# Own job lists for the first and last turns of a pipelined attention and feed-forward kernel on one core

## The chip, the core and the metric

The kernel runs on one core of one Trainium2 chip. The metric is the device time of one execution in microseconds. The engines are TensorE (PE, its weight loads PEld), VectorE (DVE), ScalarE (ACT), GpSimd (POOL) and SyncE (SP, which here only issues DMAs).

## The reference, cut to what matters

```python
def reference(x, w_qkv, b_qkv, w_out, b_out, W1, b1, W2, b2):   # x is (32, 512, 256)
    x = x + layernorm(attention(layernorm(x)))
    x = x + layernorm(relu(layernorm(x) @ W1 + b1) @ W2 + b2)
    return x
# attention: 16 heads of 16; scores = q k^T / 4 + mask; softmax; times v; times w_out
# mask: a query block of 128 rows sees its own block and block 0; block 0 sees all, all see block 0
# W1 is (256, 1024), W2 is (1024, 256), everything in float32
```

## The kernel before, in words

There are 32 batches of 512 rows. The work of one batch is cut into jobs: `x1` (transposes of the normalised input), `qk` 0 to 3 and `v` (projections), `scores_max` 0 to 19 (scores that only give a row maximum, by the DVE job `reduce`), `max_t` 0 to 3 (transposes of the maxima, copied by `copy_max`), `scores` 0 to 19 (scores again with the maximum as one more row, then `exp` on ACT), `pv` 0 to 3 (probabilities times values, read by ACT's `read_o`), `o_t`, `o2`, `op` (the output projection, read by DVE's `op_out`), `x2`, `f1` 0 to 7 and `f2` 0 to 3 (feed-forward). Each operand of a projection is held as a high and a low part (`_hi`, `_lo`), so ACT writes the high part and DVE (for h, POOL) the low one. `relu` on ACT writes h twice, `h_lo` on POOL subtracts. The layer norms are `_stats`, `_mean` (DVE), `_rstd` (POOL), `_shift`, `_apply`.

The scores' operands stand in the tile `stack`, to which SP copies q and k by 6 small DMAs for each of 8 head pairs (`load_stack` 0 to 7, line L323). The negative maxima go through DRAM: `store_row` 0 to 3 (L332) and `load_row` 0 to 3 (L336). SP issues its DMAs in order, and one that waits holds all behind it.

The order of the work is written out by hand in the table `ORDER`: one list for each engine, one turn of the pipeline, each entry a job, its number and the offset of its batch from the turn. On PE a fourth number names the pair of PSUM banks (`p_pair` 0 to 3) that the job writes; a job waits until the former user of its pair has been read out. A turn holds jobs of five batches at once. PE's program is unrolled. The other engines' programs are turns 0 to 5 written out, a loop, and the last turns written out. In the first and last turns the same list is used, and entries whose batch does not exist are left out (`there`).

The weights are loaded by SP into tiles that are free at the start and split by ACT (`w_hi`, L515 and L521) and DVE (`w_lo`, L587 and L594). POOL sets constant ones in `stack` and `values` by memsets (L726, L728) after the first layer norm's `_rstd`.

In the text a batch stands in brackets, counted from 0: max_t 0 (1) is job `max_t` 0 of the second batch.

## Time and profile before

| | us |
|---|---|
| median of 3 runs | 2061.07 (2060.56 to 2062.49) |
| profiled execution, its own time | 2061.84 |
| its span, first to last instruction | 2060.0 |

| engine | busy us | share of the span |
|---|---|---|
| PE | 1938.2 | 94% |
| PEld | 1588.0 | 77% |
| DVE | 1536.7 | 75% |
| ACT | 1408.6 | 68% |
| POOL | 722.8 | 35% |

The span is what the profiler's rows cover; 1.8 us of the execution's own time lie outside. The shares are means over a filling pipeline, a long steady middle and a draining pipeline, and the rows below take these apart. The mean granted TensorE clock was 0.977 of 2.4 GHz.

### The profile page before, as it was taken

The page shows a single profiled execution, that of the slowest core. Times are in us where ns is not written, and L with a number is a line of the kernel's source. Part 1 is how long each engine was busy: PE and PEld are TensorE (multiplying, and loading weights), DVE is VectorE, ACT ScalarE, POOL GpSimd, SP SyncE. Part 2 cuts the span into 40 slices and gives each one's busy share as a digit, 9 for nine tenths or more (in the row PEclk, how much of TensorE's full clock was granted, in tenths as well). Part 3 has the DMA queues.
Part 4 walks back from the last instruction along what each step waited for, and adds up shares of the span by engine and source line. Part 5 has one row for each costly group of instructions (what it writes and reads, how often), then busy time and mean ns, then how long its engine had stood idle before and what let it go on. Part 6 is the DMA issues. An engine that isn't in the chain of part 4 may idle for free. (4 is left out here: it accounts for less than half of the span.)

```text
span 2060.0 us, 70899 instructions
## 1 busy us (share of the span) xinstructions
PE 1938.2 (94%) x27904; PEld 1588.0 (77%) x27904; DVE 1536.7 (75%) x2916; ACT 1408.6 (68%) x2341; POOL 722.8 (35%) x905
## 2 busy tenths in 40 slices
PE   3879999999999999999999999999999999999985
PEld 2557887788888778888877888787788878778765
DVE  6577777777787777778777787877778787777631
ACT  2446677777777777777777776777777677777653
POOL 2013333333333333333333333333433334343343
PEclk8789999999999999999999999999999999999998
DMA  4343343334334333433433343343334334333200
GB/s 124 71 84 73 76 90 68 80 80 93 78 81 91 68 79 81 92 78 82 91 67 77 84 90 79 80 91 66 79 84 88 79 82 89 68 80 76 54 27 16
DMA packets 132817, 160.61 MB, mean 78 GB/s; under 512 B 29408, under 2 KB 82400, under 8 KB 132576
## 3 DMA queue, kind: packets, MB, share of 16 engines
q1 hardware_dynamic: 132048, 156.29, 35.8%
q8 instruction: 222, 3.64, 0.8%
q10 hardware_dynamic: 528, 0.52, 0.1%
q14 instruction: 19, 0.16, 0.0%
HBM read 38.21 MB, written 17.83 MB: 27 GB/s over the span
## 5 line engine op out<-in xcount | busy, mean ns | idle before, releaser
L613 DVE TENSOR_REDUCE max_bias<-p_pair 128x4 f32<-128x1024 f32 (+1 forms) x640 | 761.4, 1215 | 104.1 <-PE p_pair L363 87.9
L530 ACT ACTIVATE probs<-p_pair 128x1024 f32<-128x1024 f32 x640 | 638.8, 1027 | 246.4 <-PE p_pair L363 134.9
L746 POOL TENSOR_TENSOR h_lo<-h_f,h_hi 128x512 fp32r<-128x512 f32 x256 | 329.8, 1288 | 477.5 <-ACT h_hi L562 477.4
L366 PE MATMUL p_pair<-stack 49*128 49x256 f32 (+1 forms) x3072 | 352.3, 314 | 36.3 <-ACT probs L530 15.0
L562 ACT ACTIVATE h_f<-p_pair,b_s 128x256 f32<-128x256 f32 x512 | 247.9, 484 | 119.3 <-PE p_pair L393 119.3
L366 PEld LDWEIGHTS p_pair<-stack 49*128 49x128 f32 (+1 forms) x3072 | 241.3, 191 | 111.6 <-ACT probs L530 46.8
L393 PE MATMUL p_pair<-x_hi,w_hi 64*128 64x256 f32 (+1 forms) x2560 | 302.6, 308 | 13.0 <-DVE x_lo L625 5.5
L393 PE MATMUL p_pair<-w_hi,h_hi 64*128 64x256 f32 x2048 | 286.7, 277 | 10.0 <-POOL h_lo L746 7.4
L393 PE MATMUL p_pair<-x_hi,w_lo 64*128 64x256 f32 (+1 forms) x2560 | 295.9, 302 | 0.0
L393 PE MATMUL p_pair<-x_lo,w_hi 64*128 64x256 f32 (+1 forms) x2560 | 295.7, 302 | 0.0
L393 PE MATMUL p_pair<-w_lo,h_hi 64*128 64x256 f32 x2048 | 284.1, 274 | 0.0
L393 PE MATMUL p_pair<-w_hi,h_lo 64*128 64x256 f32 x2048 | 283.9, 274 | 0.0
L562 ACT ACTIVATE h_hi<-p_pair,b_s 128x256 fp32r<-128x256 f32 x512 | 249.1, 486 | 0.0
L363 PE MATMUL p_pair<-stack 49*128 49x512 f32 (+1 forms) x1024 | 220.2, 433 | 19.6 <-DMA stack<-qk 7.3
L393 PEld LDWEIGHTS p_pair<-x_hi,w_hi 64*128 64x128 f32 x2560 | 213.5, 187 | 24.1 <-DVE max_bias L613 13.0
L393 PEld LDWEIGHTS p_pair<-x_hi,w_lo 64*128 64x128 f32 x2560 | 215.8, 186 | 11.7
L393 PEld LDWEIGHTS p_pair<-x_lo,w_hi 64*128 64x128 f32 x2560 | 215.5, 186 | 11.7
L393 PEld LDWEIGHTS p_pair<-w_hi,h_hi 64*128 64x128 f32 x2048 | 192.9, 185 | 15.1 <-POOL h_lo L746 6.0
L432 PEld LDWEIGHTS p_pair<-probs,values 128*32 128x32 f32 x3072 | 106.3, 112 | 120.5 <-issue 81.0
L393 PEld LDWEIGHTS p_pair<-w_lo,h_hi 64*128 64x128 f32 x2048 | 193.1, 185 | 2.8
L432 PE MATMUL p_pair<-probs,values 128*32 128x256 f32 x3072 | 194.2, 385 | 0.0
L393 PEld LDWEIGHTS p_pair<-w_hi,h_lo 64*128 64x128 f32 x2048 | 192.7, 185 | 0.0
(77 smaller groups left out, 2815.6 us busy)
## 6 DMA issues: line engine op xcount, KB each, us to landing
stack<-qk SPq DMA_DIRECT2D x1536, 64.0 KB, 2.3
xr<-x SPq DMA_DIRECT2D x32, 512.0 KB, 4.0
out<-yf SPq DMA_DIRECT2D x64, 256.0 KB, 2.2
xa<-x SPq DMA_DIRECT2D x31, 512.0 KB, 4.5
shift_rows<-max_t SPq DMA_DIRECT2D x128, 8.0 KB, 1.3
stack<-shift_rows SPq DMA_DIRECT2D x128, 8.0 KB
...
```

Source lines behind the costliest of these rows:

```text
L363: last = nc.tensor.matmul(dst[:, j, :], stack[r, stationary, at, 0:P], stack[r, moving, at, :], start=True, stop=True)
L366: last = nc.tensor.matmul(dst[:, j, col:col + HALF].rearrange("p (a n) -> p a n", a=2), stack[r, stationary, at, kb * P:(kb + 1) * P], two ...
L393: last = nc.tensor.matmul(dst[:, u, cols], stationary(r), moving(r), start=part == 0 and at == 0 and m == 0, stop=part == 1 and m == adden ...
L432: last = nc.tensor.matmul(two(o, kb), v, probs[:, prob_slot(n, c), j, col:col + HALF] .rearrange("p (a n) -> p a n", a=2), start=False, st ...
L530: nc.scalar.activation(probs[:, prob_slot(quad, c), :, :], banks("scores", n)[:, :, :], ACT.Exp, scale=SCALE).then_inc(exp_done, 1)
L562: last = nc.scalar.activation(dst, banks("f1", n)[:, n % 2, u * HALF:(u + 1) * HALF], ACT.Relu, bias=b1_s[:, m:m + 1])
L613: nc.vector.tensor_reduce(dst, src, axis=AX.X, op=ALU.max, negate=True).then_inc(red_done, 1)
L746: nc.gpsimd.tensor_tensor(h_parts[1][:, m:m + 2, :], h_f[:, n % 2, :, :], h_parts[0][:, m:m + 2, :].bitcast(F32), ALU.subtract).then_inc(h ...
```

## The change

Each engine gets two more lists, `FIRST` and `LAST`, with jobs and batches written out one by one. `FIRST` stands in place of the thinned turns 0 to 3 and `LAST` in place of those after the last full turn (offsets there count from the end, -1 is the last batch). Full turns by `ORDER` run between them, 28 on PE. `ORDER` itself has other positions and other bank pairs. The jobs are the same ones; only the weight splits became jobs (`split_hi`, `split_lo`) with places in `FIRST`.

The first input comes in two halves, on ACT's and SP's queues. The weights after the first are issued from ACT's queue, each staged in a tile of its own. Of the low splits, the first stays on DVE and five go to POOL. The memset of one half of the `stack` ones runs at POOL's start, the other after both halves of the first batch are normalised.

```diff
+FIRST = {
+    "PE": [
+        ("x1", 0, 0), ("qk", 0, 0), ("qk", 1, 0), ("qk", 2, 0), ("qk", 3, 0), ("scores_max", 0, 0),
...
+        ("scores", 11, 0), ("scores", 12, 0), ("scores", 13, 0), ("o_t", 1, 0), ("scores", 14, 0),
+        ("max_t", 0, 1), ("scores", 15, 0), ("scores", 16, 0), ("pv", 2, 0), ("scores", 17, 0),
...
+    "POOL": [
+        ("ln1_rstd", 0, 0), ("ln1_rstd", 1, 0), ("ones", 0, 0), ("ln1_rstd", 0, 1), ("ones", 1, 0),
+        ("split_lo", 1, 0), ("split_lo", 2, 0), ("ln1_rstd", 1, 1), ("split_lo", 3, 0), ("ln1_rstd", 0, 2),
...
+LAST = {
+    "PE": [
...
+        ("scores", 19, -1), ("x2", 0, -2), ("o_t", 2, -1), ("pv", 3, -1), ("f1", 0, -2), ("f1", 2, -2),
+        ("f1", 1, -2), ("f1", 3, -2), ("o_t", 3, -1), ("o2", 0, -1), ("f1", 4, -2), ("f1", 6, -2),
+        ("f2", 0, -2), ("f1", 5, -2), ("f2", 1, -2), ("f1", 7, -2), ("op", 0, -1), ("op", 1, -1), ("f2", 2, -2),
+        ("f2", 3, -2), ("x2", 0, -1), ("f1", 0, -1), ("f1", 2, -1), ("f1", 1, -1), ("f1", 3, -1), ("f1", 4, -1),
+        ("f1", 6, -1), ("f2", 0, -1), ("f1", 5, -1), ("f2", 1, -1), ("f1", 7, -1), ("f2", 2, -1), ("f2", 3, -1),
...
+        W_STAGE = ((O_QKV, O_W1, probs[:, :, :, :].rearrange("p a u n -> p (a u n)")[:, 0:O_W1]),
+                   (O_WO, O_W2, h_f[:, :, :, :].rearrange("p a u n -> p (a u n)")[:, 0:KD * D]),
+                   (O_W1, O_W1 + F, ya[:, :, :].rearrange("p a n -> p (a n)")),
+                   (O_W1 + F, O_WO, o_n[:, :, :].rearrange("p a n -> p (a n)")),
+                   (O_W2, O_W2 + KB * D, x1_old[:, :, :].rearrange("p a n -> p (a n)")),
+                   (O_W2 + KB * D, WCOLS, yf[:, :, :].rearrange("p a n -> p (a n)")))
...
-            act.dma_start(xa[:, :, :], x_t[0]).then_inc(xa_in, 16)
+            act.dma_start(xa[:, 0:HB, :], x_t[0, :, 0:HB, :]).then_inc(xa_first, 16)
+            sp.dma_start(xa[:, HB:KB, :], x_t[0, :, HB:KB, :]).then_inc(xa_in, 16)
...
+                elif what == "split_lo":
+                    first_col, stop, stage = W_STAGE[n]
+                    pool.wait_ge(hi_split, n + 1)
+                    nc.gpsimd.tensor_tensor(w_lo[:, first_col:stop], stage, w_hi[:, first_col:stop].bitcast(F32),
+                                            ALU.subtract).then_inc(lo_rest, 1)
...
-                pool.wait_ge(rstd_done["ln1"], 2)
-                for j in range(2):
-                    nc.gpsimd.memset(stack[ROW * j + 32:ROW * (j + 1), 1, :, :].bitcast(F32), 1.0).then_inc(ones_set, 1)
-                    pool.wait_ge(ones_set, j + 1)
+            stack_ones(0)
+                if what == "ones" and n == 0:
+                    pool.wait_ge(norm_done["ln1"], 2)
+                    stack_ones(1)
```

What SP issues in batch 0 after the first loads stood so before (`stack<-qk x24` is `load_stack` for four pairs, `shift_rows<-max_t` is `store_row`, `stack<-shift_rows` is `load_row`):

```order
L323 DMA stack<-qk 16x2x512 x24
L332 DMA shift_rows<-max_t 16x128
L336 DMA stack<-shift_rows 2x2x512
L323 DMA stack<-qk 16x2x512 x24
L332 DMA shift_rows<-max_t 16x128
L345 DMA xa<-x 128x4x256
L336 DMA stack<-shift_rows 2x2x512
```

It stands so now:

```order
L530 DMA stack<-qk 16x2x512 x24
L539 DMA shift_rows<-max_t 16x128
L530 DMA stack<-qk 16x2x512 x6
L543 DMA stack<-shift_rows 2x2x512
L530 DMA stack<-qk 16x2x512 x6
L539 DMA shift_rows<-max_t 16x128
L530 DMA stack<-qk 16x2x512 x12
L543 DMA stack<-shift_rows 2x2x512
```

The second `store_row` moved from behind 24 DMAs of pairs 4 to 7 to behind 12 of them, and the pairs' loads stand between each store and its load.

In the middle turns PE had this around `pv` 2 (the last rows of `f2` 3 first; `stack` x2 or x4 is a `scores` or `scores_max` job, `probs,values` is `pv`, the number behind p_pair the bank pair):

```order
L393 MATMUL p_pair0<-w_hi,h_lo 128x256 x2
L363 MATMUL p_pair2<-stack 128x512 x2
L428 MATMUL p_pair3<-probs,values 32x512 x4
L432 MATMUL p_pair3<-probs,values 32x256 x4
L432 MATMUL p_pair3<-probs,values 32x2x128 x8
L377 MATMUL p_pair1<-ident,max_bias 128x64 x2
L366 MATMUL p_pair0<-stack 128x256 x4
```

It has this now:

```order
L598 MATMUL p_pair2<-w_hi,h_lo 128x256 x2
L571 MATMUL p_pair1<-stack 128x256 x4
L571 MATMUL p_pair0<-stack 128x256 x4
L568 MATMUL p_pair3<-stack 128x512 x2
L568 MATMUL p_pair2<-stack 128x512 x2
L571 MATMUL p_pair1<-stack 128x256 x4
L633 MATMUL p_pair0<-probs,values 32x512 x4
L637 MATMUL p_pair0<-probs,values 32x256 x4
L637 MATMUL p_pair0<-probs,values 32x2x128 x8
L571 MATMUL p_pair1<-stack 128x256 x4
L582 MATMUL p_pair3<-ident,max_bias 128x64 x2
```

Five score jobs now stand between `f2` 3 and `pv` 2 where one stood, and the fourth of them takes the pair that `f2` 3 has just filled.

At the program's end DVE had this (from the last `normal_o` to the statistics of the last batch's first norm; `yf<-p_pair` is `f2_out`, `ya<-p_pair` is `op_out`):

```order
L625 TENSOR_TENSOR o_lo<-p_pair,o_hi 128x2x8x64
L661 TENSOR_TENSOR ya<-p_pair,max_bias 128x1024
L683 BN_STATS bn_lny<-ya 128x6 x2
L668 TENSOR_TENSOR yf<-p_pair,b_s 128x512
L690 BN_AGGR mv_lny<-bn_lny 128x2 x2
L683 BN_STATS bn_lnf<-yf 128x6 x2
L683 BN_STATS bn_lny<-ya 128x6 x2
```

It has this now:

```order
L827 TENSOR_TENSOR o_lo<-p_pair,o_hi 128x2x8x64
L877 TENSOR_TENSOR yf<-p_pair,b_s 128x512
L894 BN_STATS bn_lnf<-yf 128x6 x2
L870 TENSOR_TENSOR ya<-p_pair,max_bias 128x1024
L901 BN_AGGR mv_lnf<-bn_lnf 128x2 x2
L894 BN_STATS bn_lny<-ya 128x6 x4
L901 BN_AGGR mv_lny<-bn_lny 128x2 x2
```

The `f2_out` of the batch before moved ahead of the last batch's `op_out`, and the two halves of the statistics stand together.

## Rows read from the trace of the kernel before

**Rows 1.** Windows by stage: busy PE, PEld, DVE, ACT, POOL; then granted clock, DMA.

```profile
0.00:180.00 180.00, 125.89 (x1240) 88.90 (x1242) 122.66 (x185) 74.80 (x96) 25.37 (x38) 0.81 0.41 89
180.00:1866.00 1686.00, 1655.44 (x24409) 1368.19 (x24406) 1330.72 (x2549) 1224.61 (x2044) 624.43 (x785) 1.00 0.39 81
1866.00:2060.00 194.00, 156.88 (x2266) 130.89 (x2262) 83.29 (x184) 109.20 (x203) 72.99 (x84) 0.93 0.17 40
```

**Rows 2.** Timeline of ACT: `x1_hi` of batches 3 and 31.

```profile
180.35 1.03 ACT L543 ACTIVATE x_hi<-p_pair 128x1024 fp32r<-128x1024 f32 x1
...
1866.89 1.03 ACT L543 ACTIVATE x_hi<-p_pair 128x1024 fp32r<-128x1024 f32 x1 [0.22 <-PE p_pair L377]
```

**Rows 3.** Timeline of all engines, first 20 us: start, duration, engine, line, operation, idle before.

```profile
8.44 7.28 DVE L705 TENSOR_SCALAR xa<-xa,mv_ln,rstd_ln 128x256 f32<-128x256 f32 x2 [0.26 <-POOL rstd_ln L739]
8.47 7.10 POOL L726 MEMSET stack<- 32x4096 f32 x2
15.63 1.09 POOL L728 MEMSET values<- 128x1148 f32 x1
15.64 1.74 DVE L587 TENSOR_TENSOR w_lo<-probs,w_hi 128x1536 fp32r<-128x1536 f32 x1
15.87 1.11 PE L377 MATMUL p_pair<-ident,xa 64*128 64x64 f32 x16 [15.87 <-DVE xa L705]
```

**Rows 4.** Timeline of SP, first 175 us.

```profile
45.20 0.35 SPq L332 DMA_DIRECT2D shift_rows<-max_t  x1
48.24 0.61 SPq L336 DMA_DIRECT2D stack<-shift_rows  x1
...
64.20 0.58 SPq L332 DMA_DIRECT2D shift_rows<-max_t  x1
...
66.03 0.54 SPq L336 DMA_DIRECT2D stack<-shift_rows  x1
...
91.72 3.81 SPq L323 DMA_DIRECT2D stack<-qk  x6
101.36 0.31 SPq L332 DMA_DIRECT2D shift_rows<-max_t  x1
```

**Rows 5.** Timeline of PE: `pv` 2 (0), then `max_t` 0 (1).

```profile
96.76 1.78 PE L428 MATMUL p_pair<-probs,values 128*32 128x512 f32 x8
...
100.74 0.27 PE L377 MATMUL p_pair<-ident,max_bias 64*128 64x64 f32 x2
```

**Rows 6.** Timeline of PE in a middle turn.

```profile
1064.09 0.74 PE L366 MATMUL p_pair<-stack 48*128 48x256 f32 x8 [0.18 <-DVE o_n L652]
```

**Rows 7.** Windows by stage, the last 88 us, columns as above.

```profile
1972.00:2015.00 43.00, 29.54 (x476) 27.36 (x478) 13.92 (x40) 19.96 (x45) 20.57 (x24) 0.96 0.12 38
2015.00:2060.00 45.00, 28.88 (x400) 26.66 (x398) 4.93 (x13) 15.18 (x37) 14.53 (x14) 0.84 0.04 13
```

**Rows 8.** Timeline of DVE, the last 80 us: `op_out`, `f2_out`, second statistics.

```profile
1984.18 1.23 DVE L661 TENSOR_TENSOR ya<-p_pair,max_bias 128x1024 f32<-128x1024 f32 x1 [7.17 <-PE p_pair L393]
...
1991.20 0.69 DVE L668 TENSOR_TENSOR yf<-p_pair,b_s 128x512 f32<-128x512 f32 x1 [5.00 <-PE p_pair L393]
...
2013.93 0.73 DVE L705 TENSOR_SCALAR xr<-xr,mv_ln,rstd_ln 128x256 f32<-128x256 f32 x2 [3.36 <-ACT x_old L569]
```

**Rows 9.** Timeline of POOL: `h_lo` 3 and 7 of the last batch.

```profile
2030.71 1.28 POOL L746 TENSOR_TENSOR h_lo<-h_f,h_hi 128x512 fp32r<-128x512 f32 x1 [0.20 <-ACT h_hi L562]
...
2046.45 1.28 POOL L746 TENSOR_TENSOR h_lo<-h_f,h_hi 128x512 fp32r<-128x512 f32 x1 [0.20 <-ACT h_hi L562]
```

**Rows 10.** The chain that ended last: start, us, engine, what, line.

```profile
2046.00 0.38 ACT h_hi L562
...
2048.81 3.02 PE p_pair L393 x48
...
2052.58 0.77 DVE bn_lnf L683 x2
2053.37 0.26 DVE mv_lnf L690 x2
...
2053.97 0.72 POOL rstd_lnf L739
```

More of the change, by code:

```diff
@@ L84 @@
+TURNS = (0, 0)
 CROSSED = ("op", "f1", "f2", "qk", "v")
@@ L228, in opens, with full_turns @@
             return what not in CROSSED or which % 2 == 0
[L230 to L239 removed]
+        def full_turns(engine):
+            offsets = [job[2] for job in ORDER[engine]]
+            return TURNS[0] - min(offsets), NB - max(offsets) - TURNS[1]
@@ new lines, in in_order @@
+        def in_order(engine):
+            start, stop = full_turns(engine)
+            return ([job[:3] for job in FIRST[engine]]
+                    + [(what, n, i + off) for i in range(start, stop) for what, n, off, *_ in ORDER[engine]]
+                    + [(what, n, NB + b) for what, n, b in LAST[engine]])
+        unit_before, last_user = {}, {}
+        for what, n, b in in_order("PE"):
+            if opens(what, n):
+                unit_before[what, n, b] = last_user.get(PAIR_OF[what, n])
+                last_user[PAIR_OF[what, n]] = what, n, b
@@ L241, in reads, with steps @@
         def reads(name, n):
             return (n // 2 + 1) * READ[name] // PRODUCTS[name] if name in CROSSED else n + 1
-        def steps(eng, jobs, job, early=None, unrolled=False):
-            def turn(i):
-                todo = [(what, n, i + off) for what, n, off, *_ in jobs if there(i + off)]
+        def steps(eng, engine, job, early=None):
+            start, stop = full_turns(engine)
+            for what, n, b in FIRST[engine]:
+                job(what, n, b)
+            for what, n, off in ORDER[engine]:
+                job(what, n, start + off)
+            with eng.Fori(start + 1, stop) as i:
+                todo = [(what, n, i + off) for what, n, off in ORDER[engine]]
@@ L251, in turn @@
                 for at, (what, n, b) in enumerate(todo):
[L252 removed]
+                    if early:
                         early(what, todo[at + 1:])
[L254 to L263 removed]
@@ L264, in steps @@
-            for i in range(NB - AHEAD, NB + BEHIND):
-                turn(i)
+                    job(what, n, b)
+            for what, n, b in LAST[engine]:
+                job(what, n, NB + b)
         def two(ap, kb):
```

445 lines of the change are left out of this document (303 added, 142 removed), and 7 rows, old and new, of tables (LAST, ORDER).

## The prediction

> **What bounds the kernel now.** I read the windows by stage first. In the middle 1686 us PE is busy for 1655.44 at a granted clock of 1.00, and DVE for 1330.72 and ACT for 1224.61, so PE sets the pace there [rows 1]. From `x1_hi` (3) at 180.35 to `x1_hi` (31) at 1866.89 lie 28 turns, 60.23 us each [rows 2]. PE idles 30.56 us in it, 1.09 a turn. The ends differ: of the first 180 us PE is busy 125.89 at a mean clock of 0.81, and DVE only 122.66; of the last 194 us PE is busy 156.88 at 0.93 [rows 1]. So 54 and 37 us of PE's idle time lie in the ends, and there the time is set by chains through other engines and SP's queue. The timelines of the ends show them.
>
> **The start, term by term**, against `x1_hi` (3) at 180.35. First, the second `ln1_apply` of batch 0 takes 7.28 us while POOL's memset of `stack` runs for 7.10; the same pair of instructions takes 0.73 elsewhere [rows 3, 8]. The change puts half of the memset at POOL's start, where DVE has nothing to do, and the other behind both applies. The transposes at 15.87 wait for this apply, and `w_lo` is queued behind it. So 7.28 - 0.73 = 6.5 us go. What DVE does beside the second memset is a TENSOR_TENSOR, and one at 15.64 ran its 1.74 us beside a memset of 1.09 [rows 3]. The input in halves I take as nothing: the first weights' split must be done as well before `qk` 0. It can bring some tenths, or lose them if the weights land later behind it. Term: -6.5.
>
> Second, SP's queue. In batch 0 `store_row` 0 is issued at 45.20 and `load_row` 0, which must wait for it, at 48.24; then, behind 24 more copies, `store_row` 1 and `load_row` 1 go at 64.20 and 66.03 [rows 4]. SP waits there 48.24 - 45.55 = 2.7 and 66.03 - 64.78 = 1.2 us with copies of q and k ready to be issued behind it, and the `scores` of the second four heads wait for that last row. `FIRST` has six copies behind each of the first two stores, so that both waits are filled. Term: -4.
>
> Third, batch 1. SP ends a copy at 91.72 + 3.81 = 95.53 and issues `store_row` 0 (1) at 101.36, 5.8 us of nothing with 24 copies behind it [rows 4]. What it waits for is `max_t` 0 (1), and that stands on PE behind `pv` 2 (0), from 96.76 to 100.74, 4.0 us at the lower clock level [rows 5]. `FIRST` has `max_t` 0 (1) ahead of it. That is 4.0, with 2 more for the waits between store and load as in batch 0. Term: -6. In batch 2 `FIRST` leaves `max_t` 0 behind `pv` 2, so only the filled waits count, and what PE gains when it idles less and keeps the upper clock level: -3.
>
> Start: 6.5 + 4 + 6 + 3 = 19.5. The bounds are wide. Below, only the first term and the row waits hold: 8. Above, DVE's 122.66 us of work plus some 5 before its first instruction cannot be passed: 52.
>
> **The middle.** The jobs are the same, so only waits can change. PE's waits there are short, as 0.18 for DVE's `o_n` [rows 6]. Read against the lists the new order moves them more than it removes them. The wait of `max_t` 1's reader among the reduces goes. But `scores` 16 now takes the pair that `f2` 3 has filled three short jobs earlier; two such jobs take 0.74 [rows 6] and DVE's `f2_out` 0.69 plus what stands ahead of it on DVE [rows 8]. Five short jobs now stand ahead of `pv` 2, each needing an `exp` or `reduce` read before its pair is free, where `f2` 3 gave them cover. The limits: nothing of PE's idle time left, -30.6; a new wait of the size of one `f2_out` each turn, +0.69 x 28 = +19. I take the middle nearer to nothing, a tenth of a microsecond a turn: -3.
>
> **The end.** From 1972 to 2015 PE is busy 29.54 of 43.00 us [rows 7], with 13.5 idle. The last batch's chain runs through it: `op_out` at 1984.18, then on DVE the first half of the statistics, then `f2_out` of the batch before, which waits 5.00 us for PE until 1991.20, and only then the second half; the last `ln2_apply` comes at 2013.93 [rows 8]. `LAST` puts `f1` and half of `f2` of batch 30 ahead of `op` (31) and the two other `f2` behind it. PE's work stays 29.5. Behind `op` the chain needs `op_out` 1.2 [rows 8], statistics twice 0.77, mean and `_rstd` 0.26 + 0.72 and an add ahead of it [rows 10], ACT's apply of about 1, POOL's add of 512 columns 1.3 as `h_lo` [rows 9], statistics, mean and `_rstd` again and DVE's apply 0.73 [rows 8]: 9, and with a handover between two engines at each of ten places some 11.5. The two `f2`, 3.02 each at their slowest [rows 10], cover 5.5 to 6 of it. So 6 us stay idle instead of 13.5: -7.5.
>
> From 2015 on: `h_lo` 3 of the last batch starts at 2030.71 and `h_lo` 7 at 2046.45, 15.7 us apart [rows 9], since `f1` 4 to 7 stand behind two whole `f2`. A `relu` is four ACT instructions, whose rows stand 0.37 apart [rows 10], so four of them need 5.9 us. `LAST` has `f1` 4 and 6 ahead of `f2` 0 and only one `f2` ahead of the last `f1`, which leaves some 10.5 us between: -5. What follows the last `f2` (`f2_out`, statistics, add, store) is unchanged. From 1926 to 1972, where `x2` (30) moved ahead, I take -1.5. End: -14, between -6 and, with all idle time of the two windows but the last 8 us gone, -21.
>
> **The sum** is 19.5 + 3 + 14 = 36.5. The profiled span of 2060.0 becomes 2023.5. Its own time was 2061.84, 1.8 above the span, and the median of the runs 2061.07, 0.8 below that; so 2061.07 - 36.5 = 2024.5.
>
> **A rule against this change.** Five low splits move from DVE to POOL. The row of 7.28 us shows that a POOL instruction can hold a DVE one for its whole length [rows 3]. POOL's splits by the row of `h_lo` (1.28 for 512 columns, rows of 1024 so 2.6) are 1.3 + 4 x 2.6 = 11.7 us [rows 9]. In `FIRST` I find no DVE apply beside them, so I count nothing. The Trainium skill, "SBUF — State Buffer", section "Who interferes with whom", says that a VectorE instruction in a two-port mode, or with two SBUF inputs against a GpSimd instruction that reads SBUF, blocks or is blocked in full. By it each of the five could hold an apply or DVE's own split, and the sum would be 36.5 - 11.7 = 24.8. The trace agrees for the memset; it shows no split on POOL.
>
> **The rivals.** (a) The forecast, 0.43: 2024.5, own range 2010 to 2037. (b) The ends fill better, 0.18: the start reaches -30, the end -18, the middle -10: 2003. For it speaks DVE's low share at the start; against it, that each batch's row must go through DRAM in series. (c) The ends give little, 0.24: -8.5 at the start (the memset and the shorter of the waits), -8 at the end, 0 in the middle, 2044.6; or, with half of each term behind the memset's, 2037 to 2044. For it speaks that a wait taken away on SP may show up on ACT or PE. (d) POOL's splits hold DVE in full, 0.05: 2061.07 - 24.8 = 2036. (e) Slower, 0.06: the wait of `scores` 16 for `f2_out`. If DVE reaches `f2_out` after `reduce`, apply and mean that stand ahead of it, it comes late by more than 0.69, and `pv` 2 waits for a `reduce` queued behind it. It decides from (33.5 + 4.1) / 28 = 1.34 us a turn on. At 1.5, that is 42 lost against 33.5 won: 2069.6. Against it: DVE is busy for 1330.72 of 1686 [rows 1], so it has 12 us a turn to catch up. (f) The lists change nothing that counts, 0.04: within 4.1 us, 0.2%, which is about what a measurement of this kernel can tell from no change. Against it stands the memset alone.
>
> **The numbers.** Faster 0.90, same 0.04, slower 0.06. The range leaves out (e), (f) and the lower part of (b): 2000 to 2046.
>
> **What would show it.** `ln1_apply` at about 0.7 us and PE's first transposes at 9 to 10 us; the first stack copy near 21; SP's wait ahead of `store_row` 0 (1) below 2 us; `x1_hi` (3) near 161; the distance to `x1_hi` (31) 28 times 60.1; from there to the end 180 instead of 193. The forecast is wrong if the turn leaves 59.9 to 60.5, if the first weights land so late that `qk` 0 starts after 14 us, or if PE's clock at the start stays at its lower level for as long as now.

## The result, and the profile after

| | median us | range | runs |
|---|---|---|---|
| before | 2060.82 | 2059.74 to 2062.49 | 6 |
| after | 2040.66 | 2040.12 to 2050.05 | 6 |

The ratio is 0.9909, with a 95% interval from 0.9891 to 0.9926, which is 0.9% faster; the two medians stand 20.2 us apart. The forecast was 36.5 us and 2024.5, so the time lies inside the range of 2000 to 2046, and 16 us above its point. Five of the six runs lie between 2040.12 and 2041.29. The one of 2050.05 shows a mean granted clock of 0.975, the others 0.978 to 0.980; the middle turns below show one thing that can differ from run to run.

First the windows by stage of the changed kernel, cut at `x1` (3) and at `x1` (31), as in [rows 1]. The columns are: stretch and length, then busy time and count of PE, PEld, DVE, ACT and POOL, the granted clock, the DMA share and GB/s.

```profile
0.00:167.00 167.00, 122.76 (x1232) 86.07 (x1234) 111.30 (x182) 75.92 (x98) 36.15 (x43) 0.83 0.44 98
167.00:1854.00 1687.00, 1651.01 (x24427) 1360.50 (x24425) 1316.34 (x2549) 1221.16 (x2044) 632.71 (x785) 1.00 0.38 81
1854.00:2039.50 185.50, 152.60 (x2258) 129.10 (x2254) 83.72 (x184) 108.96 (x204) 72.75 (x84) 0.93 0.17 41
...
1952.00:1995.00 43.00, 32.31 (x512) 28.53 (x512) 16.21 (x45) 21.72 (x47) 20.55 (x24) 0.92 0.10 31
1995.00:2039.50 44.50, 28.18 (x400) 26.42 (x400) 5.89 (x14) 15.28 (x37) 14.39 (x14) 0.81 0.04 13
```

Both ends are shorter, by 12.8 and 8.1 us between the same jobs. The middle kept its length, and it should have lost 3. Over both ends PE still idles 44 and 33 us, where before it idled 54 and 37 [rows 1]. The last two rows answer to [rows 7]: the last 88 us of the program still have 27 us of PE idle.

The timeline of ACT answers to [rows 2]:

```profile
167.59 1.03 ACT L755 ACTIVATE x_hi<-p_pair 128x1024 fp32r<-128x1024 f32 x1 [0.35 <-PE p_pair L582]
...
1854.67 1.05 ACT L755 ACTIVATE x_hi<-p_pair 128x1024 fp32r<-128x1024 f32 x1
```

And the timeline of all engines in the first 20 us answers to [rows 3]:

```profile
8.25 0.74 DVE L916 TENSOR_SCALAR xa<-xa,mv_ln,rstd_ln 128x256 f32<-128x256 f32 x2 [0.26 <-POOL rstd_ln L959]
9.05 3.51 POOL L935 MEMSET stack<- 32x4096 f32 x1 [0.83 <-DVE xa L916]
9.13 1.12 PE L582 MATMUL p_pair<-ident,xa 64*128 64x64 f32 x16 [9.13 <-DVE xa L916]
9.49 1.76 DVE L804 TENSOR_TENSOR w_lo<-probs,w_hi 128x1536 fp32r<-128x1536 f32 x1 [0.51 <-ACT w_hi L737]
12.71 1.23 PE L598 MATMUL p_pair<-x_hi,w_hi 64*128 64x512 f32 x4 [2.46 <-DVE x_lo L827]
```

The apply takes 0.74 instead of 7.28 and the transposes start at 9.13 instead of 15.87: this term is right to a few tenths. `w_lo` takes 1.76 beside the second memset, as it took 1.74 before. `qk` 0 starts at 12.71, ahead of the 14 that was the sign of late weights.

Between the same marks all kernels of this study can be compared. The marks are the starts of PE's `x1` transposes in each timeline. "Falls" counts, among the 27 turns from `x1` (4) to `x1` (31), those in which `pv` 3, all its matmuls together, takes over 2.6 us instead of 2.36; what that is comes below. Times are in us, the ratio is against the kernel before on the same chip. Marks and falls are those of the one profiled execution of each kernel, the median is that of all its runs. For e2 and e4 the profiled execution was the slowest of their runs (2061.17 of eleven, 2055.20 of five), for e10 and e11 the fastest (2041.67 and 2033.93).

| kernel | x1 (3) | x1 (4) to (31) | falls | x1 (31) to end | op (31) to x2 (31) | x2 (31) to end | median | ratio [95%] |
|---|---|---|---|---|---|---|---|---|
| before | 179.7 | 1626.7 | 0 | 193.9 | 34.0 | 45.2 | 2060.82 | 1 |
| after | 166.9 | 1627.5 | 2 | 185.8 | 18.6 | 44.3 | 2040.66 | 0.9909 [0.9891, 0.9926] |
| e1 | 168.0 | 1627.6 | 0 | 195.7 | 33.9 | 45.4 | 2055.48 | 0.9973 [0.9964, 0.9983] |
| e2 | 167.1 | 1636.8 | 7 | 195.8 | 34.0 | 48.3 | 2055.93 | 0.9974 [0.9964, 0.9985] |
| e3 | 165.0 | 1627.1 | 1 | 197.6 | 34.4 | 48.5 | 2051.75 | 0.9961 [0.9947, 0.9975] |
| e4 | 169.1 | 1637.1 | 7 | 187.4 | 18.7 | 45.9 | 2048.05 | 0.9939 [0.9927, 0.9952] |
| e5 | 166.6 | 1633.3 | 5 | 180.5 | 18.6 | 40.8 | 2038.47 | 0.9887 [0.9869, 0.9905] |
| e6 | 164.6 | 1631.8 | 3 | 187.4 | 20.1 | 44.6 | 2043.80 | 0.9915 [0.9897, 0.9933] |
| e7 | 166.4 | 1628.2 | 3 | 183.9 | 16.0 | 46.5 | 2039.55 | 0.9900 [0.9879, 0.9920] |
| e8 | 180.1 | 1740.6 | 18 | 192.4 | 18.8 | 44.3 | 2176.60 | 1.0565 [1.0541, 1.0588] |
| e9 | 177.0 | 1662.9 | 0 | 194.3 | 18.6 | 45.6 | 2096.72 | 1.0164 [1.0146, 1.0182] |
| e10 | 166.7 | 1627.1 | 2 | 186.8 | 18.6 | 46.9 | 2047.18 | 0.9931 [0.9917, 0.9945] |
| e11 | 165.1 | 1628.8 | 3 | 179.0 | 15.9 | 40.2 | 2036.89 | 0.9883 [0.9867, 0.9898] |
| e12 | 167.9 | 1628.3 | 0 | 195.9 | 15.9 | 45.4 | 2066.19 | 1.0017 [1.0007, 1.0027] |

### The profile page after: what moved, and what is told of

Its sections match the earlier page's. It is cut to its first block and busy times, and to the rows that moved or that the text cites. A ratio compares the mean times of both kernels' runs of the same rounds, so it can differ in the third digit from the quotient of the medians.

```text
span 2039.5 us, 71012 instructions
## 1 busy us (share of the span) xinstructions
PE 1926.4 (94%) x27904; PEld 1575.7 (77%) x27904; DVE 1511.4 (74%) x2913; ACT 1406.0 (69%) x2343; POOL 741.6 (36%) x910
## 5 line engine op out<-in xcount | busy, mean ns | idle before, releaser
L817 DVE TENSOR_REDUCE max_bias<-p_pair 128x4 f32<-128x1024 f32 (+1 forms) x640 | 772.8, 1222 | 262.0 <-PE p_pair L571 139.8
L571 PE MATMUL p_pair<-stack 49*128 49x256 f32 (+1 forms) x3072 | 319.6, 306 | 39.5 <-DVE max_bias L817 22.7
L571 PEld LDWEIGHTS p_pair<-stack 49*128 49x128 f32 (+1 forms) x3072 | 226.9, 188 | 126.7 <-DVE max_bias L817 59.8
L598 PE MATMUL p_pair<-w_hi,h_hi 64*128 64x256 f32 x2048 | 309.4, 279 | 5.0 <-ACT h_hi L774 2.5
L598 PE MATMUL p_pair<-w_hi,h_lo 64*128 64x256 f32 x2048 | 305.7, 275 | 0.0
L598 PE MATMUL p_pair<-w_lo,h_hi 64*128 64x256 f32 x2048 | 305.5, 275 | 0.0
L568 PE MATMUL p_pair<-stack 48*128 48x512 f32 (+1 forms) x1024 | 220.6, 438 | 23.3 <-DMA stack<-qk 9.0
L598 PEld LDWEIGHTS p_pair<-w_hi,h_hi 64*128 64x128 f32 x2048 | 217.0, 186 | 7.4 <-POOL h_lo L964 3.4
L598 PEld LDWEIGHTS p_pair<-w_lo,h_hi 64*128 64x128 f32 x2048 | 216.7, 185 | 1.2
L598 PEld LDWEIGHTS p_pair<-w_hi,h_lo 64*128 64x128 f32 x2048 | 216.9, 185 | 0.0
```

The costliest lines, as they stand in the source:

```text
L568: last = nc.tensor.matmul(dst[:, j, :], stack[r, stationary, at, 0:P], stack[r, moving, at, :], start=True, stop=True)
L571: last = nc.tensor.matmul(dst[:, j, col:col + HALF].rearrange("p (a n) -> p a n", a=2), stack[r, stationary, at, kb * P:(kb + 1) * P], two ...
L598: last = nc.tensor.matmul(dst[:, u, cols], stationary(r), moving(r), start=part == 0 and at == 0 and m == 0, stop=part == 1 and m == adden ...
L817: nc.vector.tensor_reduce(dst, src, axis=AX.X, op=ALU.max, negate=True).then_inc(red_done, 1)
```

## The experiments

### e1 to e4: which of the three lists gives what

e1 has the order and the pairs of before in `ORDER`, and first and last turns thinned from it. What stays of the change is the memsets, the input in halves, the late weights and the splits on POOL. The cuts of code in this part are read against the changed kernel: a minus is what that one has.

```diff
 ORDER = {
     "PE": [
-        ("scores_max", 16, -2, 2), ("qk", 1, -1, 3), ("scores", 6, -2, 0), ("pv", 0, -2, 1),
+        ("scores_max", 17, -2, 1), ("qk", 1, -1, 2), ("scores", 6, -2, 0), ("pv", 0, -2, 3),
...
```

> The order of before on every engine and in every turn, its ends thinned from the table as before; the halves of the memset, the input in halves and the late weights as in the changed kernel. Theory A (each part of the change carries to the end of the span): PE's first transposes move from 15.87 to 9.1 and x1_hi (3) from 180.35 to about 173.6, the turn stays 60.23 to 60.26, the end 193; time 2061 - 6.8 = 2054. Rival B (what is won before batch 0's copies is taken back by SP's queue and the lower clock level in batches 0 to 2): x1_hi (3) at 177 or later, 2058 to 2060.

e2 has the new `ORDER` and thins both ends from it; e3 has `FIRST` as changed and thins the end; e4 has `LAST` as changed and thins the start.

```diff
 FIRST = {                       # e2 and e4
     "PE": [
-        ("x1", 0, 0), ("qk", 0, 0), ("qk", 1, 0), ("qk", 2, 0), ("qk", 3, 0), ("scores_max", 0, 0),
+        ("x1", 0, 0), ("qk", 0, 0), ("qk", 1, 0), ("qk", 2, 0), ("scores_max", 0, 0), ("qk", 3, 0),
...
 LAST = {                        # e2 and e3
     "PE": [
...
-        ("f1", 7, -2), ("op", 0, -1), ("op", 1, -1), ("f2", 2, -2), ("f2", 3, -2), ("x2", 0, -1),
+        ("op", 0, -1), ("op", 1, -1), ("f2", 0, -2), ("f2", 1, -2), ("f1", 4, -2), ("f1", 6, -2),
+        ("f1", 5, -2), ("f1", 7, -2), ("f2", 2, -2), ("f2", 3, -2), ("x2", 0, -1),
...
```

> The changed kernel's order of the middle in all turns, its ends thinned from that table: no lists of their own. Against e1_old_order only the order differs. Theory A: the middle's new order is worth the 1.4 us that the two traces show between x1 (3) and x1 (30) (1626.4 before, 1625.0 after), so 1 to 2 us below e1_old_order, about 2052.5. Rival B (the new table was made for ends of their own and thins badly): up to 5 us above e1_old_order. Rival C (the middle is worth the 3 us of the forecast or more): 2051 or less.

> The changed kernel with its list for the first turns and its middle, the last turns thinned from the middle's table. Theory A (additive): start -12.8, middle -1.4, the end as before: x1_hi (3) at 167.6, the distance from x1_hi (31) to the end 193; 2061 - 14.2 = 2047. So FIRST is worth 6 us against e2_middle_only, of which the forecast had 13. Rival B: FIRST gives its whole 12.8 by the memset, that is nothing against e2_middle_only.

> The changed kernel with its list for the last turns and its middle, the first turns thinned from the middle's table. Theory A (additive): start -6.8, middle -1.4, the end -6 to -8: 2061 - 14.5 to 16.2 = 2045 to 2046.5. The turn from x1 (30) to x1 (31) took 61.9 in the changed kernel against 60.0, with a granted clock of 0.72 in 5 us of it. If the order of LAST brings that dip, it is here again; if it is the place in time, it is not. Rival B: LAST gives 14 us against e2_middle_only, as forecast, and the start takes some of it back in the changed kernel: 2038.

Measured: 2055.48, 2055.93, 2051.75 and 2048.05, with before at 2061.69. By the table, `LAST` is worth 8 us with the thinned start: from `x1` (31) to the end 195.8 without it (e2) and 187.4 with it (e4), and the medians stand 7.9 apart. With `FIRST` ahead of it the same marks give 11.8 (197.6 in e3, 185.8 in the changed kernel). `FIRST` is worth little: `x1` (3) comes at 168.0, 167.1 and 169.1 in the three kernels without it and at 165.9 in the mean of the seven with it and the new middle (after, e3, e5, e6, e7, e10, e11); e12, with it and the old middle, has 167.9. That is 2.2 us of the 13 that the terms behind the memset's gave the queue of SP and `max_t` 0 (1). The medians of e2 and e3 stand 4.2 apart, but e2's trace had seven falls in the middle and e3's one, so not all of that is the start.

So where do the 12.8 us at the start come from? 6.7 are the memset. From the first transposes to `x1` (3) it is 163.8 us before, 157.8 in the changed kernel, and 159.1, 158.3 and 160.0 in the three without `FIRST`: most of the other 6 us came without the list. The windows from one `x1` to the next show how; the third, from `x1` (2) to `x1` (3), before:

```profile
122.30:180.00 57.70, 50.50 (x600) 35.65 (x598) 43.97 (x80) 35.46 (x53) 11.51 (x17) 0.88 0.36 73
```

and in e1, which has the order of before:

```profile
113.30:168.00 54.70, 47.19 (x588) 33.75 (x586) 43.47 (x80) 35.96 (x53) 13.34 (x18) 0.94 0.39 79
```

PE's jobs are the same, and they take 3.3 us less, at a granted clock of 0.94 instead of 0.88. Over the three windows PE is busy 25.08 + 47.18 + 47.19 = 119.4 us instead of 27.18 + 48.18 + 50.50 = 125.9, each at a higher clock. The work took less time because less of it ran at the lower of the clock's two levels. The changed kernel itself has less of this: PE is busy for 122.76 of its first 167 us, 3.1 less than before, and idles 44.2 instead of 54.1, of which the memset is 6.7. Over the traces of the table PE idles 44.5 us up to `x1` (3) in the mean of the seven with `FIRST` and 47.0 in the mean of the three without. Why e1's first turns hold the upper level more is not settled: DVE is busy 4.9 us less in the first window, since the splits left it, and I made no run with the splits alone.

In the middle the traces of e2 and e4 are 9 us longer than those of e3 and the changed kernel, which have the same list there, and than e1's. That was not expected by any theory and became the subject of e8 and e9. In the medians e2 and e1, which differ in the order of the middle and in the ends thinned from it, stand only 0.5 us apart.

### e5: the last batch's second half in another buffer

After `x2` (31) only 0.9 us of the forecast 5 were won. ACT's timeline of the changed kernel shows `relu` 3 end and `relu` 4 begin:

```profile
2010.16 0.48 ACT L774 ACTIVATE h_hi<-p_pair,b_s 128x256 fp32r<-128x256 f32 x1
2018.02 0.47 ACT L774 ACTIVATE h_f<-p_pair,b_s 128x256 f32<-128x256 f32 x1 [7.37 <-PE p_pair L598]
```

PE's `f1` 4 had been done for long. The other thing that `relu` 4 waits for is `f2` 1: `h_hi` and `h_lo` hold one half of the rows, and `f2` 0 and 1 read the first half out of them. No order of the `f1` jobs shortens this. e5 puts the second half into `stack`, which nobody needs any more, and so may run all `f1` ahead of `f2`.

```diff
+        def h_of(part, b, half):
+            if isinstance(b, int) and b == NB - 1 and half == 1:
+                return stack[:, part, 0:KF // 2, :].rearrange("p q (h t) -> p (q h) t", h=2)
+            return h_parts[part]
...
-                    wait(act, mm["f2"], b, 2, half)
+                    wait(act, mm["f2"], b, 2, 0 if isinstance(b, int) and b == NB - 1 else half)
...
 LAST, PE, last batch:
-  f1 4, f1 6, f2 0, f1 5, f2 1, f1 7, f2 2, f2 3
+  f1 4, f1 6, f1 5, f1 7, f2 0, f2 1, f2 2, f2 3
```

> The changed kernel, and in the last batch alone the second half of h lies in stack, which nothing reads any more, so that relu 4 need not wait until f2 0 and f2 1 have read the first half; f1 5 and f1 7 stand ahead of f2 0. Theory A (the buffer of h, not the order of f1, kept relu 4 to 7 apart from relu 0 to 3): relu 4 follows relu 3 without the 7.37 us of waiting, h_lo 7 ends near 2018 instead of 2026 on the clock of the changed kernel, and from x2 (31) to the end it takes 39 us instead of 44.3: 5 us won, the 5 of the forecast, time near 2035.5. Rival B (the f2 jobs themselves and the lower clock level set this stretch): 0 to 2 us won.

Measured: 2038.47, and 40.8 us from `x2` (31) to the end instead of 44.3. ACT's timeline of e5 has the wait all but gone:

```profile
2017.10 0.47 ACT L785 ACTIVATE h_f<-p_pair,b_s 128x256 f32<-128x256 f32 x1 [1.59 <-PE p_pair L609]
2017.47 0.47 ACT L785 ACTIVATE stack<-p_pair,b_s 128x256 fp32r<-128x256 f32 x1
```

The buffer was the cause of the wait: in the changed kernel `relu` 4 starts right behind `f2` 1's last row, and in e5 it waits for PE's `f1` alone. e5 changed the order of `f1` along with it. The 3.5 us won behind `x2` (31) are read from the traces. The runs alone don't separate the two kernels: the medians stand 2.2 us apart, and the ratios, 0.9887 and 0.9909, have intervals that overlap.

### e6 and e7: the chain between `op` (31) and `x2` (31)

The changed kernel's chain behind `op` takes 15.2 us, from the start of `op_out` to the end of the second apply. The rows, in order of time, of DVE, POOL and ACT:

```profile
1979.86 1.23 DVE L870 TENSOR_TENSOR ya<-p_pair,max_bias 128x1024 f32<-128x1024 f32 x1 [3.02 <-PE p_pair L598]
...
1982.27 1.26 POOL L964 TENSOR_TENSOR h_lo<-h_f,h_hi 128x512 fp32r<-128x512 f32 x1
...
1982.59 0.96 DVE L906 SCALAR_TENSOR_TENSOR nmr_lnf<-mv_lnf,rstd_lnf 128x2 f32<-128x2 f32 x1
...
1985.34 1.29 POOL L974 TENSOR_TENSOR yf<-yf,x_old 128x512 f32<-128x512 f32 x1
...
1985.41 1.23 DVE L906 SCALAR_TENSOR_TENSOR nmr_lny<-mv_lny,rstd_lny 128x2 f32<-128x2 f32 x1 [0.77 <-POOL rstd_lny L959]
...
1991.92 1.42 POOL L974 TENSOR_TENSOR yf<-yf,x_old 128x512 f32<-128x512 f32 x1 [0.53 <-ACT yf L789]
...
1993.43 0.63 ACT L783 ACTIVATE x_old<-xr 128x512 f32<-128x512 f32 x1 [1.65 <-POOL yf L974]
1994.30 0.74 DVE L916 TENSOR_SCALAR xr<-xr,mv_ln,rstd_ln 128x256 f32<-128x256 f32 x2 [2.08 <-POOL rstd_ln L959]
```

Batch 30's `h_lo` and both its `final_add` stand between batch 31's adds and its statistics, and `x1_keep` (31) at 1993.43 waits for the second `final_add` (30), because there is one `x1_old` for both. The rows show a third thing: two of DVE's smallest instructions, the `_shift` on 2 columns (`nmr`) of batch 30 and then of batch 31, take 0.96 and 1.23 us where the median of the 128 is 0.15. How much of the 15.2 they make was not measured alone. Each starts inside a POOL instruction that reads SBUF and ends with it, 1982.59 + 0.96 beside `h_lo`'s 1982.27 + 1.26, and 1985.41 + 1.23 beside `final_add`'s 1985.34 + 1.29. e6 puts the last batch's jobs ahead where only the order forbids it. e7 also keeps the last batch's x1 in `xa`, which is free then, and moves the second half of batch 30's layer norm behind the last `x2`.

```diff
 LAST, POOL:                     # e6
-  h_lo 4, h_lo 5, h_lo 6, lnf_rstd 0, h_lo 7, ..., final_add 0, x1_add 0, x1_add 1
+  h_lo 4, lnf_rstd 0, h_lo 5, h_lo 6, h_lo 7, ..., x1_add 0, x1_add 1, final_add 0, ln2_rstd 0
...
+        def old_x1(b):          # e7
+            return xa if isinstance(b, int) and b == NB - 1 else x1_old
...
-                    wait(act, final, b - 1, 2, n + 1)
-                    nc.scalar.activation(x1_old[:, at, :], xr[:, at, :], ACT.Copy).then_inc(x1_kept, 1)
+                    if old_x1(b) is x1_old:
+                        wait(act, final, b - 1, 2, n + 1)
+                    nc.scalar.activation(old_x1(b)[:, at, :], xr[:, at, :], ACT.Copy).then_inc(x1_kept, 1)
```

> The changed kernel; in the last turns alone DVE, POOL and ACT take the last batch's statistics, adds and applies ahead of the ones of the batch before. Nothing else. Theory A (the second ln2_apply of the last batch waits for x1_keep 1, that for final_add 1 of the batch before, and that for f2 3, since both batches use one buffer x1_old): op (31) to x2 (31) stays at 18.6 us within 0.5, no gain. Rival B (the jobs of the batch before stand in the way on the three engines): 3 us won there, near 2037.5.

> As e6_chain_order, and the last batch keeps its x1 in xa, which is free by then, so that x1_keep need not wait for final_add of the batch before; that batch's last statistics, apply and add come behind the last x2. Theory A: op (31) to x2 (31) takes 15 us instead of 18.6, the 11.5 of the forecast and some 3.5 until its first instruction; time near 2037. Rival B (PE's f2 of the batch before and its f2_out set it): 17.5 or more.

Measured: 20.1 us from `op` (31) to `x2` (31) in e6, 16.0 in e7, 18.6 in the changed kernel; medians 2043.80 and 2039.55. The order alone gives nothing, since `x1_keep` still waits (its second copy starts at 1996.73, behind a `final_add` of 1.26 at 1995.39). With the second buffer, and with the second half of batch 30's layer norm out of the way, 2.6 us go; e7 doesn't part the two. From `x1` (31) to the end e7 is 1.9 us shorter than the changed kernel, and from `x2` (31) on it is longer, 46.5 us instead of 44.3. The rows of e7:

```profile
1978.51 1.23 DVE L880 TENSOR_TENSOR ya<-p_pair,max_bias 128x1024 f32<-128x1024 f32 x1 [2.73 <-PE p_pair L607]
...
1984.07 0.16 DVE L916 SCALAR_TENSOR_TENSOR nmr_lny<-mv_lny,rstd_lny 128x2 f32<-128x2 f32 x1 [0.69 <-POOL rstd_lny L969]
...
1986.31 0.61 ACT L793 ACTIVATE xa<-xr 128x512 f32<-128x512 f32 x1
1987.05 1.29 POOL L984 TENSOR_TENSOR yf<-yf,x_old 128x512 f32<-128x512 f32 x1
...
1990.31 0.73 DVE L926 TENSOR_SCALAR xr<-xr,mv_ln,rstd_ln 128x256 f32<-128x256 f32 x2 [0.26 <-POOL rstd_ln L969]
```

From `op_out` to the end of the apply it is now 12.5 us, `_shift` takes its 0.16 again, and one `final_add` of 1.29 still stands ahead of `_rstd`. Without it the chain would be 11.2, close to the 11.5 that was forecast for the bare chain.

### e8 and e9: what happens ahead of `pv` 3

In all nine traces with the new `ORDER` unaltered, 1 to 7 of the 27 turns are some 1.7 us longer than the others, most of them 61.6 to 61.9 us instead of 60.0 to 60.3, and each time at the same place. (A few turns of 60.4 to 61.4 stand in every trace, old order too, at the full clock; they are something else.) The windows of the changed kernel, 5 us each:

```profile
1045.00:1050.00 5.00, 4.60 (x54) 2.52 (x46) 4.90 (x13) 4.26 (x6) 1.86 (x4) 0.94 0.36 92
1050.00:1055.00 5.00, 5.00 (x58) 2.78 (x52) 3.72 (x8) 2.11 (x4) 1.27 (x1) 0.72 0.37 64
```

The granted clock falls here to its lower level of 1.2 GHz for 3 to 4 us. The timeline of PE shows what it did before:

```profile
1047.30 0.98 PE L571 MATMUL p_pair<-stack 49*128 49x256 f32 x8 [0.17 <-ACT probs L742]
...
1048.91 0.50 PE L571 MATMUL p_pair<-stack 48*128 48x256 f32 x4 [0.23 <-DVE max_bias L817]
...
1049.34 1.93 PE L633 MATMUL p_pair<-probs,values 128*32 128x512 f32 x8
```

It ran the short jobs from `scores` 17 to `scores_max` 8, with small waits between, and the first matmuls of `pv` 3 then take 1.93 us instead of 1.06. By the counts, such a turn costs some 1.7 us: one fall gives 1627.1 in e3, two 1627.5 here, seven 1636.8 in e2. e6 stands 3 us off that line, with 1631.8 for three falls. In the three traces with the old order (before, e1, e12) there is none. e1 at the same place of a turn as e2:

```profile
1416.38 1.06 PE L653 MATMUL p_pair<-probs,values 128*32 128x512 f32 x8
1417.23 1.50 PE L657 MATMUL p_pair<-probs,values 128*32 128x256 f32 x24
```

```profile
1421.75 1.93 PE L639 MATMUL p_pair<-probs,values 128*32 128x512 f32 x8
1423.46 2.08 PE L643 MATMUL p_pair<-probs,values 128*32 128x256 f32 x24
```

The orders differ ahead of it: in the old one `f2` 3 ends 36.3 us into the turn and `pv` 3 starts at 42.4, with 6.1 us between; in the new one `f2` 3 ends at 34.4, which makes 8.0 (medians over the turns; the text ahead of e9 has 6.3 and 8.1). `pv` 2, 2.4 us long, stands inside both. From its end to `pv` 3 the two are alike (3.6 and 3.7 us); what grew is the stretch ahead of it, from 0.2 to 1.9. My theory: the longer run of short jobs with their small waits lets the clock fall. e8 moves both `f2` jobs later, e9 only `f2` 3, by two short jobs, each with new pairs where the order needs them.

```diff
 ORDER, PE, e8:
-  o_t 1, f2 2, scores 12, scores 13, scores_max 2, f2 3, scores 14, scores_max 3, scores 15, scores 16, scores_max 4, pv 2
+  o_t 1, scores_max 2, scores 12, scores 13, scores_max 3, f2 2, scores 14, scores_max 4, scores 15, f2 3, scores 16, pv 2
...
 ORDER, PE, e9:
-  scores_max 2, f2 3, scores 14, scores_max 3, scores 15
+  scores_max 2, scores 14, scores_max 3, f2 3, scores 15
```

> The changed kernel with one stretch of PE's middle in another order: scores_max 2 to 4 go ahead of f2 2 and f2 3, so that f2 3 stands three jobs ahead of pv 2 and fewer short jobs in a row lead up to pv 3; other pairs of banks for them, f2_out 1 behind reduce 4 on DVE. Theory A (the granted clock falls in some turns after the run of short jobs that the new order has ahead of pv 3): no stretch of 5 us between batches 4 and 31 has a granted clock under 0.97, no turn takes 61.6 or more, the turn from x1 (30) to x1 (31) takes 60 instead of 61.9; 2 to 4 us won, near 2037.5. Rival B (the falls come from elsewhere): 2 to 7 of them as in the other runs. Rival C (the new waits, scores 16 behind reduce 4, or f2_out later, cost over 0.1 us a turn): turn of 60.2 or more, slower than the changed kernel.

> The changed kernel with f2 3 alone moved in PE's middle, two short jobs later (behind scores_max 3 instead of ahead of scores 14), eight of the short jobs behind it in other pairs, and reduce 3 ahead of f2_out 1 on DVE. The run of short jobs around pv 2 that ends at pv 3 is 0.6 us shorter, and no wait of over 0.25 us should be added. Theory A (the clock falls when PE works and waits by turns for too long ahead of pv 3; the order before has 6.3 us between f2 3 and pv 3 and no fall, this one 8.1 and 1 to 7 falls): at most one fall in batches 4 to 30, 2 to 4 us won. Rival B (the length of the run does not matter, the waits in it do): 2 to 7 falls as now if the waits stay, more if they grow; same time or slower.

Measured: both slower, 2176.60 and 2096.72. In e8 the pairs now serve a waiting reader at many places; the view of PE's waits between 400 and 1900 us (line waited for: total, times, longest) has

```profile
PE p_pair L577 <- DVE max_bias L823: 29.8, 53, 1.3
PE p_pair L577 <- ACT probs L748: 28.0, 72, 0.6
```

and `pv` 3 falls in 18 of 27 turns. In 20 turns the clock falls (also or instead) some 31 us into the turn; only 3 of the 27 have neither fall. The median turn is 64.9 us. A window at that place, where PE waits 0.57, 0.41 and 0.56 us ahead of the fall:

```profile
660.00:665.00 5.00, 3.94 (x39) 3.52 (x40) 2.89 (x9) 3.50 (x7) 2.12 (x3) 0.76 0.31 57
```

In e9 one wait dominates, that of `scores` 14, which takes the pair that `scores_max` 2 has just filled and that `f2` 3 used to cover:

```profile
PE p_pair L577 <- DVE max_bias L823: 45.6, 73, 1.3
```

Its turn is 61.4 us, but no `pv` 3 of its 27 falls, although PE idles 2.6 us a turn; the clock falls once in the 27 turns, in `f2` 3, right behind a wait of 1.3 us. From `f2` 3 to `pv` 3 it is 6.8 us in e9 and 6.4 in e8, both shorter than the 8.0 of the changed kernel, with no fall there in e9 and with 18 in e8. So the length of the run alone is not what decides: my theory, as it was put, does not hold for e8. What e8 has more of is waits, such as one of 0.63 us shortly ahead of `pv` 3. That the waits decide is likely from this, and not proved, since each kernel changed more than one thing. As versions they are of no use; `x1` (3) comes at 180.1 and 177.0 in them, so their pairs cost time in the first turns too. The wait in e9 is of the kind that rival (e) of the prediction described: one job without its cover costs 1.3 us a turn, near the 1.34 from which that rival decides.

### e10: SP's rows in the first turns

In the changed kernel the wait before `store_row` 0 (1) is gone, as forecast, but two others came. The timeline of SP, which answers to [rows 4]:

```profile
66.58 12.09 SPq L530 DMA_DIRECT2D stack<-qk  x18
82.63 0.32 SPq L539 DMA_DIRECT2D shift_rows<-max_t  x1
...
93.72 8.24 SPq L530 DMA_DIRECT2D stack<-qk  x12
105.63 0.31 SPq L539 DMA_DIRECT2D shift_rows<-max_t  x1
```

SP waits 4.0 us ahead of `store_row` 3 (0) at 82.63 and 3.7 ahead of `store_row` 1 (1) at 105.63. e10 puts `max_t` 3 (0) ahead of `pv` 1 (0) on PE and the last copies of batch 1 ahead of `store_row` 1 (1) on SP.

```diff
 FIRST, PE:
-  scores_max 3 (1), pv 1 (0), max_t 3 (0), scores_max 4 (1)
+  scores_max 3 (1), max_t 3 (0), pv 1 (0), scores_max 4 (1)
 FIRST, SP:
-  load_stack 6 (1), store_row 1 (1), load_row 1 (1), load_stack 7 (1)
+  load_stack 6 (1), load_stack 7 (1), store_row 1 (1), load_row 1 (1)
```

> The changed kernel; in the first turns alone PE takes max_t 3 of batch 0 ahead of pv 1, and SP issues the last six copies of batch 1 ahead of store_row 1. SP waited 4.0 us ahead of store_row 3 (0) and 3.7 ahead of store_row 1 (1) in the changed kernel. Theory A (these two waits took the place of the one of 5.8 that the change removed): x1 (2) and x1 (3) come 2 to 4 us earlier, 109 and 163 instead of 112.6 and 166.9; time 2037 to 2039. Rival B (SP's waits are not on the path; PE's work at the lower clock level and its short waits for DVE and ACT are): x1 (3) within 1 us of 166.9, no gain.

Measured: `x1` (3) at 166.7, as in the changed kernel (166.9). The SP rows of e10:

```profile
82.44 0.32 SPq L545 DMA_DIRECT2D shift_rows<-max_t  x1
...
94.99 12.48 SPq L536 DMA_DIRECT2D stack<-qk  x18
107.58 1.18 SPq L545 DMA_DIRECT2D shift_rows<-max_t  x1
```

The first store did not come earlier, because its reader `copy_max` 3 stands on DVE behind `qk_lo` and reduces of batch 1. The second wait did go, 107.47 to 107.58, and brought nothing: this wait of SP is not on the path. The median, 2047.18, is above the changed kernel's by 6.5 with no difference between their traces of over 2.6 us at any mark; the profiled execution, the fastest of the five, had a span of 2039.9. Like the run of 2050.05, it says that the same list runs some us apart, and I can't say from the traces that it is the falls.

### e11 and e12: the parts put together

e11 is the changed kernel with the edits of e5 and e7 both. e12 has e11's tail, the order and the pairs of before in the middle, and the changed kernel's `FIRST` with its own pairs.

```diff
+EARLY_PAIR = {                  # e12
+    ("scores_max", 16): 2, ("qk", 1): 3, ("scores", 6): 0, ("pv", 0): 1, ("scores", 7): 0, ("scores_max", 17): 3,
...
+        def pair_of(what, which, b):
+            unit = which - which % 2 if what in CROSSED else which
+            if isinstance(b, int) and (what, unit, b) in EARLY:
+                return EARLY_PAIR[what, which]
+            return PAIR_OF[what, which]
```

> The edits of e5_h_elsewhere and e7_chain_buffer together on the changed kernel. If the two waits are separate and in series, the gains add: x1 (31) to x2 (31) 137.5 us instead of 141.4 and x2 (31) to the end 41 instead of 44.3; 7 us below the changed kernel, about 2033.5, and faster than both kernels. If the clock falls for longer behind the shorter chain, some of it is lost, as the 46.5 of e7_chain_buffer behind x2 (31) shows: 2036.

> The middle's order of before (all five engines and its pairs of banks), the changed kernel's list for the first turns with the pairs that it has there, and e11_both_buffers' order from the last batch's pv 3 on with its two buffers; the last turns before that thinned from the middle's table. Theory A (the new order of the middle has waits as short as the old one's, and its falls of the granted clock, 1 to 7 in each trace, are what it loses): no stretch of 5 us between batches 4 and 31 under 0.97, as in both traces of the old order; x1 (4) to x1 (30) 1566 to 1568 us against a mean of 1571 over the traces of the new order; x1 (3) at 167 within 2; the end as in e11_both_buffers within 3. Time 2032 to 2036, at or below e11_both_buffers. Rival B (the falls come with the lists of the ends or with the time of the first turns): 1 to 7 falls here too. Rival C (the list of the first turns does not fit the old middle): x1 (4) 3 us or more later.

Measured: e11 2036.89, ratio 0.9883 [0.9867, 0.9898]. It has the lowest time of all, though its interval touches that of the changed kernel. From `x1` (31) to the end it takes 179.0 us, where the forecast said 180 for the change itself. The window of its last 40 us, in which PE idles 13.4, where in the changed kernel it idles 16.3 in the last 44.5:

```profile
1992.00:2032.00 40.00, 26.58 (x400) 25.61 (x400) 6.91 (x18) 16.38 (x39) 16.72 (x17) 0.84 0.06 21
```

e12 was meant to have the best of each and came out at 2066.19, slower than before. Its middle has no fall, but the seams between lists of different orders and pairs cost more: from `x1` (3) to `x1` (4) it takes 72.5 us where the others take 59.2 to 59.8 (e8 and e9 aside). The first row of PE's waits between 178 and 245 us (2.2 for one of ACT's `h_hi` comes next) is

```profile
PE p_pair L644 <- ACT probs L818: 2.8, 2, 1.6
```

and at the other seam `x2` (30) waits 5.49. In the last batch one `f1` waits 4.69 for ACT's `relu` where e11's waits 1.70: the pairs of the old middle don't fit the new end. So e12 doesn't tell whether the old middle would be better with the new ends; it tells that `FIRST` and `LAST` only fit the `ORDER` they were found with.

## Why the prediction was right or wrong

The outcome is that of rival (c), whose own range was 2037 to 2044: the ends give less. Of the 36.5 us, 16.3 did not come in the medians and 16.0 in the traces: 6.7 at the start, 3.4 in the middle, 5.9 at the end. That the time is inside the range is in part luck: 3.1 us of those won at the start are PE work that ran at a higher clock, which the sum held only as a side remark.

**Right.** The memset term: 6.7 for a forecast of 6.5, in it two tenths from the input in halves (the first statistics start at 5.05 instead of 5.24). The wait before `store_row` 0 (1) gone. Rival (d), POOL's splits holding DVE in full, did not come in its size. The first two of the five splits on POOL ran beside DVE's reduces without stretching them:

```profile
31.66 1.26 POOL L951 TENSOR_TENSOR w_lo<-h_f,w_hi 128x512 fp32r<-128x512 f32 x1
32.88 2.40 POOL L951 TENSOR_TENSOR w_lo<-ya,w_hi 128x1024 fp32r<-128x1024 f32 x1
...
31.44 4.62 DVE L817 TENSOR_REDUCE max_bias<-p_pair 128x2 f32<-128x1024 f32 x4 [0.68 <-PE p_pair L568]
```

Four reduces in 4.62 are 1.16 each, no more than their mean of 1.22 over the whole kernel. The Trainium skill, "SBUF — State Buffer", section "Who interferes with whom", says that `tensor_reduce` on trn2 never contends with GpSimd; the trace agrees. The fifth split is different, and it is the case that the prediction's rule against the change describes:

```profile
126.92 2.40 POOL L951 TENSOR_TENSOR w_lo<-yf,w_hi 128x1024 fp32r<-128x1024 f32 x1
128.23 1.10 DVE L906 SCALAR_TENSOR_TENSOR nmr_lny<-mv_lny,rstd_lny 128x2 f32<-128x2 f32 x1
```

DVE's `_shift`, which reads two tiles in SBUF, takes 1.10 us instead of 0.15 and ends with the split, at 129.3. So the mechanism of rival (d) is real and cost 1 us of DVE here, once in five splits. It also works where the prediction did not look for it: in the kernel before 31 of the 128 `_shift` are stretched so, 30 of them beside `h_lo`, and 5 in the changed kernel.

**Start, the terms behind the memset's (-4, -6, -3).** These failed in kind. They read SP's waits as time on the path. Those waits went and two others came, but the list is worth 2.2 us in all instead of 13, and e10 takes one more such wait away without moving `x1` (3). The other part of the 6 us came without the list, in e1 as less time at the clock's lower level (125.9 us of PE work became 119.4; in the changed kernel 122.8). It was in the prediction only as a side remark to batch 2.

**The middle (-3).** Without falls, the nine traces give 1624.6 on average from `x1` (4) to `x1` (31) (their lengths less 1.7 for each fall), against 1627.5 in the mean of the three with the old order, so -2.9, which is the size that was forecast. But the falls, on average 3.7 of them, give back 6.2, and the mean of the nine is 1630.9. The prediction read the clock of 1.00 of the middle as given. The step that failed is "the jobs are the same, so only waits can change". Nor are the -2.9 shown to be waits. The windows from `x1` (4) to `x1` (31), before and after:

```profile
239.50:1866.10 1626.60, 1596.94 (x23546) 1319.70 (x23544) 1283.61 (x2458) 1181.06 (x1972) 602.51 (x757) 1.00 0.39 81
```

```profile
226.30:1853.80 1627.50, 1592.28 (x23550) 1312.10 (x23548) 1269.05 (x2458) 1177.96 (x1972) 611.04 (x757) 1.00 0.38 81
```

PE idles 35.2 us in the changed kernel and 29.7 before, and is busy 4.7 us less, with two falls in it. A short job's row is longer when PE waits behind it than when the next job follows (0.50 us against some 0.24 to the next start), so part of a wait counts as busy, and these rows don't say what shortened the turn. The effect on the median is less sure still: e2 and e1 stand 0.5 us apart.

**The end, first term (-7.5, chain of 11.5).** The mechanism was right and the size off. From `op` (31) to `x2` (31) PE idled 12.1 us before and 9.1 now, where 6 were forecast. The chain was summed as if batch 31 had the engines for itself, 11.5; it takes 15.2, since batch 30's `final_add` and `h_lo` stand in it, hold DVE's `_shift` twice, and `x1_keep` waits for `x1_old`. e7 brings it to 12.5. Another part came where the prediction had put only -1.5: from `x1` (31) to `x2` (31) 148.7 us became 141.4, with 4.2 less of idle, 3.0 of them behind `op`, and 3.1 less of PE's busy time, at a granted clock of 0.97 instead of 0.96.

**The end, second term (-5).** It came to -0.9. The step "`f1` 4 to 7 stand behind two whole `f2`" named the order as the cause, and the cause was the buffer: `relu` 4 waits for `f2` 1 in either order. e5 gives it another one and wins 3.5 more. With both repaired, e11 reaches the 180 that was forecast.
